# Probabilities times values in an attention and FFN kernel: one matmul over block-diagonal probabilities, or two 64-row matmuls into two PSUM banks

## The reference

```python
x = x + xattn(layernorm(x), ctx, ctx, pos, mask, Wq, Wk, Wv, Wo)
x = x + ffn(layernorm(x), weight, bias, gate_w, in_channel_scale, out_channel_scale)
# xattn: q, k with rotary embedding; softmax(q k^T / sqrt(128), masked) v; times Wo
attn = softmax(where(mask == 0, -1e9, einsum('bhqd,bhkd->bhqk', q, k) / sqrt(D)))
x = einsum('bhqk,bhkd->bhqd', attn, v)
# ffn: per token mixed input and output scales around x @ sign(weight).T
```

## Time and profile before

| | |
|---|---|
| median of 3 runs | 1342.0 us (1341.62 to 1342.18) |
| span of the profiled execution, first to last instruction | 1338.7 us |
| PE busy | 1252.5 us, 94% |
| PE weight loads | 1029.8 us, 77% |
| DVE busy | 1178.2 us, 88% |
| ACT busy | 687.8 us, 51% |
| POOL busy | 594.5 us, 44% |
| HBM traffic | 79 GB/s over the span |

### The profile page before, as it was taken

The page is one execution under the profiler, slowest core; times in us unless marked ns, Lnnn a source line. Parts: engine busy times, 40 slices in busy tenths (PEclk is TensorE's granted clock), DMA queues, the critical chain, the costliest instruction groups (busy, mean ns, idle before and its releaser), DMA issues.

```text
span 1338.7 us, 21655 instructions
## 1 busy us (share of the span) xinstructions
PE 1252.5 (94%) x6228; PEld 1029.8 (77%) x6228; DVE 1178.2 (88%) x2071; ACT 687.8 (51%) x1384; POOL 594.5 (44%) x435
## 2 busy tenths in 40 slices
PE   6799999999999999999899999999999999999977
PEld 5677777877777788777788877887777788877765
DVE  7799999889999999998899999999889999988864
ACT  4555555544555554455554455554555554455522
POOL 5244434333445444544333564443444444454324
PEclk9799999999999999999899999999999999999977
DMA  7233332222322222332222332223232212222100
GB/s 211 60 99 106 96 89 73 72 69 77 107 79 72 67 80 64 115 98 75 86 59 63 94 92 65 78 76 89 78 88 79 64 55 71 71 87 79 47 1 32
DMA packets 136916, 105.86 MB, mean 79 GB/s; under 512 B 12776, under 2 KB 111080, under 8 KB 136864
## 3 DMA queue, kind: packets, MB, share of 16 engines
q1 hardware_dynamic: 131488, 94.78, 24.5%
q10 hardware_dynamic: 4608, 8.39, 1.8%
q0 software_dynamic: 768, 2.10, 0.5%
HBM read 101.05 MB, written 4.19 MB: 79 GB/s over the span
## 4 chain that ended last, share of the span: by engine, by line
PE 61%; DVE 25%; issue 7%; ACT 4%; POOL 0%; DMA 0%; DVEq 0%; ACTq 0%; POOLq 0%; SPq 0%
PE chunk L1018 14%; PE chunk L1020 14%; PE chunk L1019 13%; PE sc_ps L1062 8%; DVE swp L771 6%; DVE qT L783 4%; DVE rot L770 4%; DVE kT L783 4%; ACT swp L467 3%; PE tr_ps L1007 3%; DVE pT_lo L702 2%; PE aux L1007 2%; PE o_ps L1020 1%; PE o_ps L1018 1%; PE o_ps L1019 1%
## 5 line engine op out<-in xcount | busy, mean ns | idle before, releaser
L384 POOL TENSOR_TENSOR w_lo<-raw,w_hi 128x512 fp32r<-128x512 f32 x192 | 268.7, 1410 | 555.3 <-ACT w_hi L467 555.2
L384 POOL TENSOR_TENSOR wo_lo<-raw,wo_hi 128x512 fp32r<-128x512 f32 x132 | 219.0, 1669 | 40.2 <-ACT wo_hi L467 40.2
L1018 PE MATMUL chunk<-wo_hi,oT_hi 128*128 128x512 f32 x512 | 211.1, 412 | 0.0
L467 ACT ACTIVATE swp<-chunk 64x512 f32<-64x512 f32 x320 | 190.0, 594 | 29.6 <-DVE qT L783 19.0
L1020 PE MATMUL chunk<-wo_hi,oT_lo 128*128 128x512 f32 x512 | 201.8, 394 | 0.0
L1019 PE MATMUL chunk<-wo_lo,oT_hi 128*128 128x512 f32 x512 | 201.1, 393 | 0.0
L1018 PE MATMUL chunk<-xT_hi,w_hi 128*128 128x512 f32 (+1 forms) x512 | 200.2, 391 | 0.0
L1020 PE MATMUL chunk<-xT_hi,w_lo 128*128 128x512 f32 (+1 forms) x512 | 199.9, 390 | 0.0
L1019 PE MATMUL chunk<-xT_lo,w_hi 128*128 128x512 f32 (+1 forms) x512 | 199.6, 390 | 0.0
L495 ACT ACTIVATE probs<-probs 128x256 f32<-128x256 f32 x128 | 53.5, 418 | 227.9 <-DVE probs L729 227.9
L467 ACT ACTIVATE pT_hi<-tr_ps 64x256 fp32r<-64x256 f32 x256 | 96.7, 378 | 129.6 <-PE o_ps L1020 115.3
(11 more groups left out here) (266 smaller groups left out, 2326.1 us busy)
## 6 DMA issues: line engine op xcount, KB each, us to landing
raw<-in_L_xattn_Wo SPq DMA_DIRECT2D x132, 256.0 KB, 2.6
raw<-in_L_xattn_Wq SPq DMA_DIRECT2D x128, 256.0 KB, 2.7
raw<-in_L_xattn_Wk SPq DMA_DIRECT2D x32, 256.0 KB, 2.8
raw<-in_L_xattn_Wv SPq DMA_DIRECT2D x32, 256.0 KB, 2.7
acc<-in_x ACTq DMA_DIRECT2D x16, 256.0 KB, 2.7
c_tile<-in_ctx SPq DMA_DIRECT2D x12, 256.0 KB, 3.3
x_tile<-in_x SPq DMA_DIRECT2D x12, 256.0 KB, 3.7
result<-y ACTq DMA_DIRECT2D x12, 256.0 KB, 2.0
```

The costliest lines, as they stand in the source:

```text
L384: nc.gpsimd.tensor_tensor(lo, raw[:, n % RING, :], hi.bitcast(F32), ALU.subtract).then_inc(wsplit_lo, 1)
L467: return nc.scalar.activation(dst, src, ACT.Copy)
L1018: nc.tensor.matmul(bank, a_hi, b_hi, start=i == 0, stop=False)
```

## The change

Each batch gets matmuls of its own. `pT_hi` and `pT_lo` lose their second half: one instruction of 128 partitions copies, one subtracts, and no zeros are needed. `values` issues six matmuls of 64 rows and 256 columns, two for each of the three products: batch 0 on partitions 0 to 63 into the first bank, batch 1 on partitions 64 to 127 into the second. Each bank is used in half. The two banks are now one tensor `o_both` that every tile fills, so `values(p)` waits for `out_lo(p - 1)`. `out_hi` and `out_lo` read 256 columns out of each bank in one instruction, 512 columns as before.

```diff
-        pT_hi, pT_lo = (sb(n, [P, 2, 2 * P], F32R) for n in ("pT_hi", "pT_lo"))
+        pT_hi, pT_lo = (sb(n, [P, 2 * P], F32R) for n in ("pT_hi", "pT_lo"))
...
-        o_ps = [stack.enter_context(nc.psum_tensor(f"o_ps{i}", [P, 512], F32)) for i in range(2)]
+        o_both = stack.enter_context(nc.psum_tensor("o_ps", [P, 2, 512], F32))
+        o_ps = [o_both[:, i, :] for i in range(2)]
...
+        def heads_of_o():
+            return o_both[:, :, 0:HG * S].rearrange("p b (h s) -> p b h s", h=HG)
...
-            for zeros in (gate_raw[:, :], in_raw[:, :], out_raw, route[:, :], pT_hi[:, :, :].bitcast(F32), pT_lo[:, :, :].bitcast(F32)):
+            for zeros in (gate_raw[:, :], in_raw[:, :], out_raw, route[:, :]):
...
-                copy(pT_hi[0:S, 0, :], tr_ps[0:S, 0:2 * P])
-                copy(pT_hi[S:P, 1, :], tr_ps[S:P, 0:2 * P]).then_inc(pT_h, 1)
+                copy(pT_hi[:, :], tr_ps[:, 0:2 * P]).then_inc(pT_h, 1)
...
-                lo_of(pT_lo[0:S, 0, :], tr_ps[0:S, 0:2 * P], pT_hi[0:S, 0, :])
-                lo_of(pT_lo[S:P, 1, :], tr_ps[S:P, 0:2 * P], pT_hi[S:P, 1, :]).then_inc(pT_l, 1)
+                lo_of(pT_lo[:, :], tr_ps[:, 0:2 * P], pT_hi[:, :]).then_inc(pT_l, 1)
...
                 pe.wait_ge(pT_l, n + 1)
-                if not (s.first_attn and p < 2):
-                    pe.wait_ge(o_lo, n - 1)
-                split_products(o_ps[p % 2][:, :], [(v_hi[:, p, :], v_lo[:, p, :], flat2(pT_hi), flat2(pT_lo))]).then_inc(pv_done, 1)
+                if not (s.first_attn and p == 0):
+                    pe.wait_ge(o_lo, n)
+                for i, (v, probs_of) in enumerate(((v_hi, pT_hi), (v_hi, pT_lo), (v_lo, pT_hi))):
+                    for b in range(2):
+                        keys = slice(b * S, (b + 1) * S)
+                        last = nc.tensor.matmul(o_both[:, b, 0:HG * S], v[keys, p, :], probs_of[keys, :],
+                                                start=i == 0, stop=i == 2)
+                last.then_inc(pv_done, 1)
```

More of the change, by code:

```diff
@@ L509, in out_hi @@
                     act.wait_ge(outproj_done, (s.U - 2) * PAIRS + p + 1)
-                copy(oT_hi[:, p, :, :].rearrange("p h (b s) -> p b h s", b=2),
-                     o_ps[p % 2][:, :].rearrange("p (b h s) -> p b h s", b=2, h=HG)).then_inc(o_hi, 1)
+                copy(oT_hi[:, p, :, :].rearrange("p h (b s) -> p b h s", b=2), heads_of_o()).then_inc(o_hi, 1)
             def swap(s, j):
@@ L750, in pT_lo_split @@
                 dve.wait_ge(pT_h, (s.U - 1) * PAIRS + p + 1)
-                lo_of(pT_lo[0:S, 0, :], tr_ps[0:S, 0:2 * P], pT_hi[0:S, 0, :])
-                lo_of(pT_lo[S:P, 1, :], tr_ps[S:P, 0:2 * P], pT_hi[S:P, 1, :]).then_inc(pT_l, 1)
+                lo_of(pT_lo[:, :], tr_ps[:, 0:2 * P], pT_hi[:, :]).then_inc(pT_l, 1)
             def out_lo(s, p):
                 dve.wait_ge(o_hi, (s.U - 1) * PAIRS + p + 1)
-                lo_of(oT_lo[:, p, :, :].rearrange("p h (b s) -> p b h s", b=2),
-                      o_ps[p % 2][:, :].rearrange("p (b h s) -> p b h s", b=2, h=HG),
+                lo_of(oT_lo[:, p, :, :].rearrange("p h (b s) -> p b h s", b=2), heads_of_o(),
                       oT_hi[:, p, :, :].rearrange("p h (b s) -> p b h s", b=2)).then_inc(o_lo, 1)
```

## The result

The changed kernel takes **1467.8 us** (median of 4 runs, 1461.42 to 1471.47), the one before 1341.8 us in the same series (1338.31 to 1342.18): ratio 1.0942, 95% interval 1.0918 to 1.0966. It is slower by 126 us. The forecast was 1502 us, in a range of 1434 to 1550.

A forecast was written before the change was run, and what follows sets the result against it. TensorE was taken to set the pace, 94% busy. The profiled span of 1338.7 us plus 125 for slots, 1 for the last slot and 34 for the clock gave 1498.7; with 3.3 above the span, 1502 us, range 1434 to 1550.

The forecast's parts named there:

- the ring: Each values product waits for the previous out_lo, behind swap and rotation: 125 us over 31 slots, 1 us for the last.
- V1: Product values(1), now waiting for out_lo(0) behind soft_b(3) on DVE: starts 0.87 us later in a bare slot.
- V1 to V2 and V2 to V3: Spacing of values(1), values(2) and values(3): 6.26 us each, +2.59 and +2.41; rotate(1) taken at 3.63, upper end 4.58.
- V3 to the last projection: From values(3) to the slot's last projection: 7.86 us becomes 6.3, the 1.45 us rotation stall gone, gain 1.55.
- Slots: Whole-slot sum for bare slots, taken the same for intake slots: +4.32 us each, 19 slots.
- The FFN slot: Slot with an FFN tile: +3.22 us from values(1) to the last projection, +0.4 before it; +3.6, 12 slots.
- The products: Six 256-column matmuls per values call: left at 0.77 us to the next matmul, bounds 0.40 and 1.1.
- the forecast's dear bound: Upper bound for one values call: 1.1 us, with a TensorE drain at either side.
- The clock: Two new 2.6 us PE stalls a slot make the clock fall in most slots: 1.1 us a slot, 34 us.
- the one with a steady clock: Rival: the same chain of waits between products, without new clock falls: 1468 us, chance 0.22.
- the one with halves side by side: Rival: both row halves run together, values takes 0.40 us: 1434 us, or 1468 with clock falls; chance 0.22.
- The rival on the faster side: At values(2)'s wait on out_lo(1): if that ended early enough, PE would stay the bound, 1251 us; chance 0.02.

The follow-up runs named there:

- filled stalls: The changed kernel with eight unused 512-column matmuls into an empty bank ahead of the third and the fourth product of values: 1455.7 us, ratio 1.0848.

## Why the prediction was right, and which sizes were off

The direction, the place and the mechanism held: the ring V, `pT_hi`, swap, rotation, `out_lo`, next V, twice a slot. The number was 34 us too high. Term by term, for the bare slot at 299.80:

- **V1**: +0.87 forecast; V1 starts 16.35 us into the slot against 15.50 before, +0.85.
- **V1 to V2 and V2 to V3**: 6.26 forecast each, 6.10 and 6.12 measured. The 3.63 us of rotation and `out_lo` came as 3.60 in both, so the lower figure was right for rotate(1) too: its product with the sine table no longer meets GpSimd. V1 to `pT_hi` was 0.72 and not 0.92.
- **V3 to the last projection**: 6.3 forecast, 6.15 measured, a gain of 1.71 for my 1.55.
- **Not in my sum**: 0.34 us from the last projection to the end of the slot (6.30 before, 6.64 now), all of it at the wait for GpSimd's `wo_lo`: the matmul at 337.59 starts 0.58 us behind the one ahead of it, 0.35 more than the pitch of 0.23. The chain has 12% of POOL in it now, which was 0%.
- **Slots**: +4.32 forecast; +4.18 in the bare slot and +4.1 in the intake slot shown above, in neither of which the fall costs anything. These two were right within 0.2 us.
- **The FFN slot** was mis-sized: +3.6 forecast, +2.9 to +3.0 measured. In the slot at 562.32 V1 moved by 0.37 us, as forecast (0.4); V1 to the last projection is 20.49 us for my 21.02, so the part over the rings was 0.5 us too dear.
- **The products** were the term that I left at 0.77 within 0.40 to 1.1. From the first pair to the second it is 0.20 us, 0.12 to the third and 0.23 to the next matmul, 0.55 in all; that next matmul then takes 0.34 us to its successor in place of 0.23. My reason against a smaller value was the 0.10 us pitch of short matmuls applied to six of them, but the two matmuls of a pair start together (0.003 us apart at V1 here). So the halves do run side by side, which was a rival with a chance of 0.22, at the wrong size (0.40), and the forecast's dear bound, time lost at either side, is there too, in part.
- **The clock** was the largest miss: 34 us forecast, 12 measured. I priced a fall at 6.83 us at half rate from the earlier trace rows. In the steady state of the changed kernel each fall but one lasts 3.41 us, as in the two rows above. A fall came in 26 of the 31 slots. Those that begin behind the first stall, as the one at 323.57, cost nothing or little: its slot, at 41.36 us, is as long as the slot of 41.40 us with filled stalls, and where the fall begins within about 0.2 us behind the start of V2 the slot is 0.2 to 0.3 us longer. The half-rate projection eats the second stall (0.95 us are left of 2.5), as the forecast said it would, but I had still charged 0.8 us for it, for a V2 at half rate, and V2 at 322.25 runs ahead of the fall. Those at the second stall or behind it, as the one at 1207.62, cost 1.36 us (45.21 against 43.85), not 3.4. There are eight such slots, seven of 1.3 to 1.5 us and one, with the long fall, of 2.9, and these make up the 12 us. The clock is at 0.50 for 9% of the span, just below the 10 to 20% that I named as a sign.

Altogether: ring 126 forecast and 116 measured, clock 34 and 12, and 1.7 us around the span in place of 3.3. That is the whole of the 34 us.

Two rivals had 1468 us, the measured number, and neither was right as a mechanism: the one with a steady clock had no falls, and the one with halves side by side had the full shrinkage and 34 us of falls, two errors that cancel. The rival on the faster side named `out_lo(1)` as the place. It was one of the places: moving it alone took the stall from V2 (1428.9 us), and only with output 2 moved as well did the time come below 1342 (1325.8). The order of no queue changes in this change, so its 0.02 was fair.

## What to carry to other kernels

A wait for another engine's step costs what stands ahead of that step in its queue, not what the step takes: the same semaphore wait cost 193 us or 9 us by where three short steps on each of two engines stood. When a change trades double buffering for cheaper work, move the step that frees the buffer ahead of everything that isn't needed for it, all links of the ring at once, and judge the change only then; here it turned 1468 us into 1311, below the 1342 of before. Price a clock fall by what lies behind it: in front of another stall it cost 0 to 0.3 us here, behind the last one 1.3 us and more. So taking away one of two stalls can bring less than that stall was long. And measure a shorter group of matmuls from the matmul ahead of it to the second one behind it: 0.55 us in place of 0.68 came with 0.2 us more around it.

## What the hardware showed that I had not expected

- 64-row matmuls of the two row halves start together: the second pair of 256 columns 0.20 to 0.22 us behind the first, the third 0.12 us behind the second. A matmul of the second half starts ahead of two that were issued before it for the first.
- Between 128-row matmuls such a group loses some 0.1 us ahead of it (V3) and 0.1 us behind it, so six of 256 columns took PE no less time than three of 512 (1.21 against 1.13 us).
- PE idle for 2.2 to 2.3 us ahead of V2, and for up to 2.5 us ahead of V3, was followed by a fall to 0.50 in 26 of 31 slots. Before, the stalls of 1.45 us in the steady state never were the earlier trace rows.
- Filling stalls with matmuls whose results nobody reads took 12 us off a kernel.

One thing was not tried. Putting both batches of a pair into one bank, or using the column halves of both banks in turn, would bring the alternation back. The Trainium skill ("PSUM — Partial Sum Buffer", PSUM bank collisions raise a hardware error) says that different row tiles may not write one bank at the same time, and that an engine may not read a bank while TensorE writes it, other columns included; no run here shows it.
